# A narrow block for the last SwiGLU chunk on two column tiles, and second products dealt out behind the ups

## The reference, cut to what matters

```python
approx_out = ...                       # seven Taylor terms, a product each
ffn_out = (silu(x @ ffn_gate_w.T) * (x @ ffn_up_w.T)) @ ffn_down_w.T   # F = 1248
x = layernorm(x + approx_out + ffn_out)
# second layer: xf @ c1_w.T @ c2_w.T -> the winner of each block of 32 of 1792 columns,
# h = relu(w1[winner] . xf), out = sum of h * w2t[winner]
x = layernorm(x + out)
```

## Time and profile before

| | us |
|---|---|
| median of 3 runs | 713.79 |
| the profiled execution's own time | 714.67 |
| its span (first to last instruction) | 712.9 |
| PE busy | 704.6 (99%) |
| DVE busy | 527.2 (74%) |
| POOL busy | 291.0 (41%) |
| ACT busy | 269.5 (38%) |

### The profile page before, as it was taken

The page is one execution under the profiler, slowest core; times in us unless marked ns, Lnnn a source line. Parts: engine busy times, 40 slices in busy tenths (PEclk is TensorE's granted clock), DMA queues, the critical chain, the costliest instruction groups (busy, mean ns, idle before and its releaser), DMA issues.

```text
span 712.9 us, 10308 instructions
## 1 busy us (share of the span) xinstructions
PE 704.6 (99%) x3949; PEld 380.7 (53%) x3949; DVE 527.2 (74%) x977; ACT 269.5 (38%) x455; POOL 291.0 (41%) x276
## 2 busy tenths in 40 slices
PE   9999999999999999999999999999999999999996
PEld 3444444444444444444444456666666666667763
DVE  5989897796887778677787988958885778337235
ACT  1575457435721121221222234444334333443342
POOL 0462443211111161244215576897366435743331
PEclk9999999999999999999999999999999999999999
DMA  9546309401000110110010222121224101220101
GB/s 338 251 145 195 60 15 378 81 14 46 2 15 17 22 22 2 28 27 20 6 16 19 50 50 50 29 66 17 49 75 64 47 4 60 62 46 1 60 2 60
DMA packets 40545, 44.67 MB, mean 63 GB/s; under 512 B 25008, under 2 KB 32816, under 8 KB 39600
## 3 DMA queue, kind: packets, MB, share of 16 engines
q1 hardware_dynamic: 37808, 39.29, 18.6%
q0 software_dynamic: 2112, 4.19, 3.3%
q10 hardware_dynamic: 576, 0.52, 0.2%
HBM read 34.33 MB, written 4.42 MB: 54 GB/s over the span
## 4 chain that ended last, share of the span: by engine, by line
PE 85%; issue 1%; DVE 1%; ACT 1%; POOL 1%; DVEq 0%; ACTq 0%
PE acc L545 31%; PE pb L525 15%; PE pa L525 15%; PE pb L791 10%; PE pa L791 8%; PE acc L631 2%; PE acc L880 2%; PE pick_b L697 1%; PE pick_a L697 1%; POOL big L1160 1%; PE pick_a L682 0%; ACT work L1120 0%; PE pick_b L880 0%; PE pick_b L541 0%; PE acc L541 0%
## 5 line engine op out<-in xcount | busy, mean ns | idle before, releaser
L545 PE MATMUL acc<-big,work 128*128 128x512 f16 x1038 | 235.1, 379 | 0.0
L1151 POOL TENSOR_TENSOR work<-work 128x512 f16<-128x512 f32 x90 | 107.6, 1206 | 273.7 <-ACT work L1023 213.7
L545 PEld LDWEIGHTS acc<-big,work 128*128 128x128 f16 x1038 | 101.6, 98 | 115.4
L525 PE MATMUL pa<-xs,big 128*128 128x512 f16 x480 | 111.2, 379 | 0.0
L525 PE MATMUL pb<-xs,big 128*128 128x512 f16 x480 | 110.1, 379 | 0.0
L1890 DVE TENSOR_TENSOR pa<-pa,big 128x512 f32<-128x512 f32 x28 | 19.6, 699 | 79.6 <-ACT big L1103 68.6
L525 PEld LDWEIGHTS pa<-xs,big 128*128 128x128 f16 x480 | 46.1, 98 | 54.1
L525 PEld LDWEIGHTS pb<-xs,big 128*128 128x128 f16 x480 | 46.0, 98 | 53.4
L631 PE MATMUL acc<-big 128*128 128x512 f16 x328 | 72.0, 379 | 0.2
L1023 ACT ACTIVATE work<-work 128x512 f16<-128x512 f32 x40 | 25.3, 631 | 111.0 <-DVE work L1617 111.0
L1160 POOL TENSOR_TENSOR big<-work,big 128x512 f16<-128x512 f32 x27 | 36.7, 1375 | 63.3 <-ACT big L961 63.1
(11 more groups left out here) (235 smaller groups left out, 988.1 us busy)
## 6 DMA issues: line engine op xcount, KB each, us to landing
big<-in_w_all SPq DMA_DIRECT2D x2, 3840.0 KB, 18.0
big<-in_x_t SPq DMA_DIRECT2D x16, 256.0 KB, 6.3
rows<-in_x POOLq DMA_DIRECT2D x4, 1024.0 KB, 12.0
big<-spread_rows SPq DMA_DIRECT2D x16, 256.0 KB, 6.1
big<-in_w_all SPq DMA_DIRECT2D x2, 1536.0 KB, 11.4
big<-spread_rows SPq DMA_DIRECT2D x16, 192.0 KB, 5.1
out<-rows SPq DMA_DIRECT2D x3, 1024.0 KB, 4.4
big<-in_w_all SPq DMA_DIRECT2D x1, 2048.0 KB, 14.6
```

The costliest lines, as they stand in the source:

```text
L525: mm = nc.tensor.matmul(dst[:, :], weights(wp)(kc * P, P), x_part16(g, xp, kc), start=(kc == 0 and wp == xp), stop=(kc == KC - 1 and wp == 1))
L545: mm = nc.tensor.matmul(acc[t][:, :], act_part(pair, j, ap, t * P, P), weights(wp)(0, H), start=(first and ap == wp), stop=(last and ap == 1))
L1151: nc.gpsimd.tensor_tensor(act_part(pair, j, 1), act32[j], act_part(pair, j, 0), ALU.subtract).then_inc(act_lo, halves)
```

## The change

Two things are changed. First, the last chunk's weights are laid out anew on the host (and this chunk is now second in its group, after chunk 8). Its gate slot holds 64 gate columns and 64 up columns, its up slot holds the other 32 of each and 64 zeros. The gate product stays 12 matmuls of 128 x 512 and gives both halves for 64 columns. The up product becomes `narrow_product`: 24 matmuls of 64 weight columns by 256 tokens, in turn on the left and the right half of PE's columns, one half for each half of the tokens. ACT and DVE take this chunk in pieces, and its second product uses 96 partitions in place of 128.

Second, in groups 1 to 3 the two second products no longer stand together behind a pair: the first goes behind the first up product of the pair (`halfway`), the second stays. The fourth score product moves behind the second of them, and in a group's first pair the third does too. DVE's `moments` of a group are cut in two around a L1617.

```diff
@@ PE
+            def narrow_product(dst, weights, g):
+                for kc in range(KC):
+                    for wp, xp in ((0, 0), (0, 1), (1, 0)):
+                        for h in range(2):
+                            side = slice(h * WIDE, (h + 1) * WIDE)
+                            mm = nc.tensor.matmul(dst[side, h * HT:(h + 1) * HT], weights(wp)(kc * P, WIDE),
+                                                  x_part16(g, xp, kc, h * HT, HT), start=(kc == 0 and wp == xp),
+                                                  stop=(kc == KC - 1 and wp == 1), tile_position=(0, h * WIDE))
+                return mm
@@ unit1
-                    if not (start and j == 0):
+                    if u == 1 and j == 0:
+                        pe.wait_ge(tail_taken, g + 1)
+                    elif not (start and j == 0):
                         pe.wait_ge(silu_ready, n)
...
+                    if u == 0 and j == 1:
+                        narrow_product(pb, lambda part: w1_part(s, 1, part), g).then_inc(up_ready, 1)
+                        return
                     split_product(pb, lambda part: w1_part(s, 1, part), g).then_inc(up_ready, 1)
+                    if halfway is not None and j == 0:
+                        halfway()
@@ down
-                    if j == 0 and scored is not None:
+                    if scored is not None and j == 1:
+                        if kind == "last":
+                            scores(scored, 2, pick_a)
                         scores(scored, 3, pick_b)
@@ group1
-                    unit1(g, u, t(u - 1), (g - 1, u - 2))
-                    down(g, u, "middle", t(u - 1))
+                    unit1(g, u, t(u - 1), (g - 1, u - 2), halfway=lambda: down(g, u, "middle", js=(0,)))
+                    down(g, u, "middle", t(u - 1), (1,))
@@ ACT, the last chunk
+                        act.activation(act32[j][0:WIDE], pa[0:WIDE, :], ACT.Silu, scale=gate_out[0:WIDE, bass.ds(g, 1)]).then_inc(tail_silu, 1)
+                        act.wait_ge(up_ready, n + 1)
+                        for h in range(2):
+                            last = act.activation(act32[j][WIDE:TAIL, h * HT:(h + 1) * HT], pb[h * WIDE:h * WIDE + NARROW, h * HT:(h + 1) * HT],
+                                                  ACT.Silu, scale=gate_out[h * WIDE:h * WIDE + NARROW, bass.ds(g, 1)])
+                        last.then_inc(silu_ready, 1)
@@ DVE
+            def swiglu_tail_wide(g):
+                dve.wait_ge(tail_silu, g + 1)
+                v.scalar_tensor_tensor(out=act32[1][0:WIDE], in0=pa[WIDE:P, :], ...).then_inc(tail_taken, 1)
+            def swiglu_tail_narrow(g):
+                ...   # waits up_ready, silu_ready, tail_taken; two of 32 x 256 from pb; then swiglu_ready
@@ DVE unit1
                 pick(tile, 0, pick_a)
+                if u == 0:
+                    swiglu_tail_wide(g)
+                    swiglu_tail_narrow(g)
                 pick(tile, 1, pick_b)
                 pick(tile, 2, pick_a)
-                swiglu(g, u, 1)
+                if u:
+                    swiglu(g, u, 1)
@@ DVE first_unit1
-                moments(g - 1, 1)
+                moments(g - 1, 1, (0, 1))
                 swiglu(g, 1, 0)
+                moments(g - 1, 1, (2, 3))
                 normalise(g - 1, x1_ready, low=g * TPG - TPG)
```

More of the change, by code:

```diff
@@ L529, in split_product, with second_product @@
                 return mm
-            def second_product(pair, j, weights, first, last, done=None, free=None, halved=False):
+            def second_product(pair, j, weights, first, last, done=None, free=None, halved=False, depth=P):
                 for t in range(TPG):
@@ L544, in second_product @@
                     for ap, wp in ((0, 0), (0, 1), (1, 0)):
-                        mm = nc.tensor.matmul(acc[t][:, :], act_part(pair, j, ap, t * P, P), weights(wp)(0, H),
+                        mm = nc.tensor.matmul(acc[t][:, :], act_part(pair, j, ap, t * P, P)[0:depth], weights(wp)(0, H)[0:depth],
                                               start=(first and ap == wp), stop=(last and ap == 1))
@@ L698, in scores, with unit1 @@
                                  start=True, stop=True).then_inc(score_ready, 1)
-            def unit1(g, u, tile=None, own=None, start=False, converted=False, after_gate=None):
+            def unit1(g, u, tile=None, own=None, start=False, converted=False, after_gate=None, halfway=None):
                 for j in range(2):
@@ L719, in unit1, with down @@
                         pe.wait_ge(w1_lo, 3 * n + 2)
+                    if u == 0 and j == 1:
+                        narrow_product(pb, lambda part: w1_part(s, 1, part), g).then_inc(up_ready, 1)
+                        return
                     split_product(pb, lambda part: w1_part(s, 1, part), g).then_inc(up_ready, 1)
+                    if halfway is not None and j == 0:
+                        halfway()
                     if tile is not None and j == 1:
                         scores(tile, 2, pick_a)
-            def down(g, u, kind, scored=None):
+            def down(g, u, kind, scored=None, js=range(2)):
                 before = g * U1 + u - 1
-                for j in range(2):
+                for j in js:
                     m = before * 2 + j
@@ L733, in down @@
                                    done=down_ready if last else None,
-                                   free=(lambda t: added(1, g - 1, t)) if first else None)
-                    if j == 0 and scored is not None:
+                                   free=(lambda t: added(1, g - 1, t)) if first else None,
+                                   depth=(TAIL if u == 1 and j == 1 else P))
+                    if scored is not None and j == 1:
+                        if kind == "last":
+                            scores(scored, 2, pick_a)
                         scores(scored, 3, pick_b)
@@ L765, in _ @@
                 group1(g)
-                unit1(g + 1, 0, g * TPG - 1, (g - 1, TPG - 1))
-                down(g + 1, 0, "last", scored=g * TPG - 1)
+                unit1(g + 1, 0, g * TPG - 1, (g - 1, TPG - 1), halfway=lambda: down(g + 1, 0, "last", js=(0,)))
+                down(g + 1, 0, "last", g * TPG - 1, (1,))
             group1(GROUPS - 1)
@@ L1022, in swiglu @@
                     act.wait_ge(swiglu_ready, n + 1)
-                    act.activation(act_part(pair, j, 0), act32[j], ACT.Copy).then_inc(act_hi, 1)
+                    depth = TAIL if tail else P
+                    act.activation(act_part(pair, j, 0)[0:depth], act32[j][0:depth], ACT.Copy).then_inc(act_hi, 1)
                     if slots is not None:
@@ L1322, in w1_max, with w1_low @@
                                      apply_absolute_value=True))
-            def w1_low(d0, d1):
+            def w1_low(d0, d1, parts=range(3)):
                 for d in range(d0, d1):
                     s = C1 - 1 - d
-                    for k in range(3):
+                    for k in parts:
                         dve.wait_ge(w1_hi, 3 * d + k + 1)
@@ L1618, in swiglu @@
                                        op0=ALU.mult, op1=ALU.mult).then_inc(swiglu_ready, 1)
+            def swiglu_tail_wide(g):
+                dve.wait_ge(tail_silu, g + 1)
+                v.scalar_tensor_tensor(out=act32[1][0:WIDE], in0=pa[WIDE:P, :], scalar=up_out[0:WIDE, bass.ds(g, 1)], in1=act32[1][0:WIDE],
+                                       op0=ALU.mult, op1=ALU.mult).then_inc(tail_taken, 1)
+            def swiglu_tail_narrow(g):
+                n = g * C1 + 1
+                dve.wait_ge(up_ready, n + 1)
+                dve.wait_ge(silu_ready, n + 1)
+                dve.wait_ge(tail_taken, g + 1)
+                for h in range(2):
+                    at = h * WIDE + NARROW
+                    r = act32[1][WIDE:TAIL, h * HT:(h + 1) * HT]
+                    last = v.scalar_tensor_tensor(out=r, in0=pb[at:at + NARROW, h * HT:(h + 1) * HT], scalar=up_out[WIDE:TAIL, bass.ds(g, 1)],
+                                                  in1=r, op0=ALU.mult, op1=ALU.mult)
+                last.then_inc(swiglu_ready, 1)
             def row(g, t):
@@ L2034, in padded @@
         return np.pad(w, pad)
-    gate, up = (chunks_first(padded(a(w), 0)).reshape(P, C1, H) for w in (L0_attn_ffn_gate_w, L0_attn_ffn_up_w))
+    gate, up = (chunks_first(padded(a(w), 0)).reshape(P, C1, H).copy() for w in (L0_attn_ffn_gate_w, L0_attn_ffn_up_w))
     down = padded(a(L0_attn_ffn_down_w), 1).T.reshape(C1, P, H).transpose(1, 0, 2)
+    ends = [w[:, C1 - 1].reshape(P, KC, P).copy() for w in (gate, up)]
+    spare = np.zeros((P, KC, P - 2 * NARROW), np.float32)
+    gate[:, C1 - 1] = np.concatenate([w[:, :, :WIDE] for w in ends], axis=2).reshape(P, H)
+    up[:, C1 - 1] = np.concatenate([w[:, :, WIDE:TAIL] for w in ends] + [spare], axis=2).reshape(P, H)
+    gate, up, down = (w[:, [*range(C1 - 2), C1 - 1, C1 - 2]] for w in (gate, up, down))
     w1 = chunks_first(a(L0_ffn_w1)).reshape(P, C2, H)
```

38 lines of the change are left out of this document (29 added, 9 removed).

## The result

The changed kernel takes 715.69 us, the median of 7 runs (715.3 to 717.59), beside 713.9 us for 7 runs of the kernel before (713.44 to 714.28): ratio 1.003, 95% interval 1.0019 to 1.0042. It is slower by 1.8 us; the forecast's main case was 715.5. The profiled execution took 715.57 us, its span 713.8.

The account below looks back on a forecast made before the run. PE, busy throughout, was taken to bound the kernel. Gains of 2.45 us against waits of 0.90, 2.18 and 1.10 turned 714.67 into 716.40 us for a profiled execution, a median of 715.5; range 711.0 to 719.9.

Parts of the forecast that it names:

- PE bounds, and waits decide: Second stage: PE is busy throughout, so only PE work that goes and new waits can move the time.
- N = 1.6: Narrow product, once per group: 1.6 us in place of 2.59, column tiles side by side plus two ends; PE saves 0.99 each.
- Rival 3: Narrow product: the column tiles run in turn, N = 2.95, giving 719.8 us; chance 0.17.
- Group 0: -0.80: Group 0: next gate product waits for DVE to take the up half out of `pa`; 0.80 us saved.
- Groups 2 and 3, first pair: -0.33 each: DVE's pieces delay pick 1, so PE waits 0.65 us before the fourth score; 0.33 saved in place of 0.99, twice.
- Pairs 9, 12 and 14: 0.30 each: Third pick meets POOL's sum instruction, so the next up product waits 0.30 us; 0.90 lost in all.
- Pair 19: 2.18: End of second stage: later picks meet POOL, so the third stage's first `pb` waits; 2.18 us lost.
- Rival 1: Pair 19: third L1750 asks 0.25 us earlier and goes ahead of POOL's L1232; wait 0.6, 713.9 us; chance 0.15.
- rival 2: Pairs 9, 12, 14 and 19: POOL doesn't hold the third pick to its instruction's end; 712.2 us; chance 0.18.
- Pairs 11 and 16: 0.55 each: DVE's `normalise` starts later, transposes land late, and the z product waits 0.55 us, twice; 1.10 lost.
- The sum: Whole change: 714.67 + 0.90 + 2.18 + 1.10 - 2.45 = 716.40 us for an execution like the profiled one; median 715.5.
- Rival 4: Whole change: DVE is never late and all four narrow products give 1.28 us; 708.7 us; chance 0.05.

Follow-up runs that it names:

- e1: Changed kernel with both second products together behind the pair again and third and fourth scores in their old places, narrow product kept; 712.65 us, ratio 0.9979.
- e4: e1 with DVE's three pieces of the narrow chunk behind the second pick in place of ahead of it; 710.11 us, ratio 0.9944.
- e5: e4 with the narrow product's 24 matmuls issued as 12 on the first column tile, then 12 on the second, not alternating; 713.64 us, ratio 0.9999.
- e6: Changed kernel with POOL's lower subtraction of the w sums (L1267) issued as three instructions of a third each; 715.59 us, ratio 1.0025.
- e2: Kernel before with only the second products split around the pair and the fourth score moved, no narrow product; 716.58 us, ratio 1.004.

## Why the prediction was right, point by point

**PE bounds, and waits decide.** Right: in this stage no transfer or engine other than DVE, for 0.4 us SP's transposes and for 0.08 us ACT (group 0) shows up, and e1 to e4 move the time by the waits that each takes away.

**N = 1.6.** It is 1.53: side by side at 0.109 us a pair, as I had it, and the two ends are 0.12 (the way in and the longer first step) and 0.10 in place of 0.16 each. Rival 3 (N = 2.95) falls by the 1.43 us, and e5 shows what order of the list would have brought much of it about. The rule that it could rest on (the Trainium skill, TensorE: Matmul & The Clock Gate, The mechanism: loads hide under running matmuls only where the row group differs) isn't borne out here: 24 loads of 110 ns, 2.64 us one after the other, pass while PE needs 1.43 for the 24 matmuls, all on the same rows.

**Group 0: -0.80.** It was -0.76. The gate product starts behind DVE's wide piece, at 114.80, 0.20 late, where I had worked out 0.19; 0.87 were saved up to there. Another 0.08 goes at pair 1's second gate product, which starts at 120.07 and not at 119.99, behind ACT's Silu of that pair (119.33 to 120.02). That wait wasn't in the prediction.

**Groups 2 and 3, first pair: -0.33 each.** The step that was mis-sized most. The wait before the fourth score is 1.33 us by starts, not 0.65, and turns the gain of 0.33 into a loss of 0.30. DVE's rows in pair 10, from the second gate product's start at 264.91:

```profile
267.89 0.62 DVE L1793 TENSOR_REDUCE big<-pick_a 128x14 f32<-128x448 f32 x1 [4.22 <-PE pick_a L710]
...
270.29 0.75 DVE L1658 SCALAR_TENSOR_TENSOR work<-pa,sc,work 64x512 f32<-64x512 f32 x1
271.17 0.98 DVE L1670 SCALAR_TENSOR_TENSOR work<-pb,sc,work 32x256 f32<-32x256 f32 x2
...
272.18 0.62 DVE L1793 TENSOR_REDUCE big<-pick_b 128x14 f32<-128x448 f32 x1
272.84 0.62 DVE L1795 TENSOR_TENSOR big<-pick_b,big 128x448 f16<-128x448 f32 x1
...
273.52 0.36 PE L710 MATMUL pick_b<-c_stack,big 128*128 128x448 bf16 x1 [1.17 <-DVE big L1795]
```

Pick 0 starts at 2.98, as forecast. The wide piece comes at 5.38 (forecast 5.26), takes 0.88 to the next start (0.66), and the two small ones take 1.01 (0.74): pick 1 starts at 7.27 in place of 6.66. What came out short were the distances to the next start, not the lengths. The straight line gave a small piece 0.46 us, and one takes 0.48; but the next start comes 0.50 after it, not 0.37. The wide piece takes 0.75, as its full-width row does, and what follows it waits for its semaphore `tail_taken`, where what follows a L1652 (0.66 after it) waits for nothing of it; that this makes the difference is likely but not tested. e4 shows that all of it hangs on their place ahead of pick 1: behind it they cost nothing.

**Pairs 9, 12 and 14: 0.30 each.** Two were (0.28 and 0.31), one 0.13. The third L1804 in pair 9 is held as said: it starts 0.88 us into POOL's instruction (0.87 by the prediction's 260.40 and 259.53) and ends 0.25 us after it. In pair 12 POOL's instruction stands earlier, 0.33 us ahead of the next pair's first gate product (305.79, 306.12) against 0.19 in pair 9 (256.46, 256.65), so it also ends 0.14 earlier. e6 removes all three waits.

**Pair 19: 2.18.** It was 1.92, with 1.94 by starts at the wait itself. The place, the releaser and the cause are as forecast; the rows:

```profile
421.74 1.64 POOL L1267 TENSOR_TENSOR big<-quad,big 128x768 f16<-128x768 f32 x1
421.74 1.47 PE L814 MATMUL pa<-xs,big 128*128 128x256 f16 x12
...
422.61 1.02 DVE L1804 TENSOR_TENSOR big<-big,rev_wide 128x448 f16<-128x448 f16 x1
...
424.20 0.74 DVE L1652 SCALAR_TENSOR_TENSOR work<-pb,sc,work 128x512 f32<-128x512 f32 x1
...
424.99 0.83 PE L814 MATMUL pb<-big,first_sums 128*128 128x256 f16 x6 [1.78 <-DVE work L1652]
```

POOL's instruction begins 0.87 us ahead of DVE's, not 0.25: POOL didn't keep its place in the earlier trace rows but came 5.93 us after the pair's first score, where I had 6.16, and DVE asked 0.4 later than I had it. POOL's earlier end accounts for the 0.24 by which the wait is shorter. Rival 1, a port missed by a hair, was therefore further off than it looked. In e2, where POOL starts 0.24 us ahead, the 1.64 of the forecast stands:

```profile
422.76 1.64 POOL L1234 TENSOR_TENSOR big<-quad,big 128x768 f16<-128x768 f32 x1
423.00 1.64 DVE L1752 TENSOR_TENSOR big<-big,rev_wide 128x448 f16<-128x448 f16 x1
```

One 0.24, one 0.87 late, and both end 0.24 to 0.25 after POOL. With e6 this settles rival 2 too. The Trainium skill (SBUF — State Buffer, SBUF: two separate sides), by which the later engine waits for the whole instruction, agrees with these rows.

**Pairs 11 and 16: 0.55 each.** 0.36. Counted from pair 10's first up product, the transposes were in fact 0.5 us later than forecast, but the z product that wants them was 0.6 later as well, by the wait in pair 10 that I had too small: the two errors nearly cancel here, by luck.

**The sum.** +2.14 in place of +1.73: too much by 0.26 in pair 19, 0.17 in pair 12 and 0.38 at the z products, too little by 1.26 in the first pairs of groups 2 and 3, the rest within 0.1. The medians differ by 1.8, and that 715.69 lies only 0.2 from the forecast is in part luck: a cost of 1.26 us that was missed stands against 0.81 of costs put too high.

**Rival 4** (DVE never late, 708.7) is not what happened, but e4 comes near it, at 710.11, by removing the reasons for being late; what is left is N = 1.53 in place of 1.31, four times, and 0.3 in group 0.

## What to carry to other kernels

On an engine that is full from end to end, moving its work saves nothing: it can only add waits, and what it adds is to be read from how late each releaser is already. When new work lands on a helping engine, first ask which of its results the full engine wants next, and place the new work behind that; here it turned a gain of 1.2 us into 3.7. Price an instruction by its distance to the next start, not by its length, and take that distance from a row in which the next instruction waits for the same thing: here the lengths were right to 0.02 us, and the distances 0.13 to 0.22 short for each piece.

## What was not expected of the hardware

- The weights of a 64-column matmul load no faster than those of a full one (the prediction's estimate was 53 ns); the row of L559's weight loads (ns, min/median/max) against 98 ns for 128 columns:

```profile
L559 PEld LDWEIGHTS pb<-xs,big x96: 106/110/110, 113.2 to 351.7; 128*64 128x64 f16 x96
```

- Two column tiles alternated in the list give 12 x 0.109 us and 0.22 at the two ends, 1.53 us, for what takes 2.33 + 0.10 one tile after the other; in that order the second tile began with three matmuls of the first still to start.
- DVE's operation on 32 x 256 elements took 0.48 us and that on 64 x 512 0.75 us, as much as 128 x 512: the free size sets the time, not the partitions.
- Three POOL subtractions of 128 x 256 took 2.07 us with DVE let in behind the second and 1.93 without (at 438.13 in e6), one of 128 x 768 1.64: 0.15 us for each of the two cuts, before any meeting with DVE.
